# Order of ScalarE's copies, the second maximum and VectorE's normalisation in a five-stage attention kernel

## The reference

```python
def attn(xq, xc, Wq, Wk, Wv, Wo, bo):            # 16 heads of 64
    q, k, v = xq @ Wq, xc @ Wk, xc @ Wv          # by heads
    return softmax(q k^T * 64 ** -0.5) v @ Wo + bo

x = attn(ln(x, g1, b1), ln(x, g1, b1), ...) + x   # SELF
x = attn(ln(x, g2, b2), ctx, ...) + x             # CROSS
x = (a * gelu(gate)) @ Wf + bf + x                # GEGLU; a, gate = split(ln(x, g3, b3) @ Wp + bp)

q, k, v = x @ Wq + bq, ctx @ Wk + bk, ctx @ Wv + bv   # CROSS2, 16 heads of 8
out = softmax(q k^T * 8 ** -0.5) v @ Wo + bo
h = gelu((ln(out) * g + b) @ W1 + b1)              # FFN
return x + out + h @ W2 + b2
```

## Time and profile before

| | |
|---|---|
| median of the runs | 475.29 us |
| the profiled execution | 476.33 us, its span 474.6 us |
| TensorE matmuls busy | 457.4 us, 96% |
| VectorE busy | 361.2 us, 76% |
| ScalarE busy | 281.6 us, 59% |
| GpSimd busy | 193.2 us, 41% |
| mean granted TensorE clock | 0.993 |

### The profile page before, as it was taken

How to read it: one execution, slowest core, us unless ns; L and a number is a source line. 1 busy time by engine, 2 the same in 40 slices (tenths; PEclk the granted TensorE clock), 3 DMA queues, 4 the chain that set the end, 5 groups by cost and what they waited for, 6 DMA issues and landing times.

```text
span 474.6 us, 17652 instructions
## 1 busy us (share of the span) xinstructions
PE 457.4 (96%) x7650; PEld 416.3 (88%) x7650; DVE 361.2 (76%) x654; ACT 281.6 (59%) x505; POOL 193.2 (41%) x216
## 2 busy tenths in 40 slices
PE   7779999999999999999999999998999999998897
PEld 7779898998998989989899898998999787777797
DVE  4868788787877887878878788796885678688562
ACT  4455654766546666566565654754554567676773
POOL 3642433445523535435442443334351323132483
PEclk9979999999999999999999999999999999999999
DMA  7101120310200000000000000000000000000011
GB/s 225 44 5 49 35 80 4 74 47 3 59 5 1 11 12 1 12 7 5 12 3 11 11 1 11 3 3 2 2 0 8 19 10 18 2 2 1 1 44 45
DMA packets 17300, 10.57 MB, mean 22 GB/s; under 512 B 7888, under 2 KB 16272, under 8 KB 17232
## 3 DMA queue, kind: packets, MB, share of 16 engines
q1 hardware_dynamic: 16800, 9.48, 7.3%
q10 hardware_dynamic: 432, 0.07, 0.1%
HBM read 8.50 MB, written 1.05 MB: 20 GB/s over the span
## 4 chain that ended last, share of the span: by engine, by line
PE 84%; DVE 10%; ACT 2%; issue 2%; POOL 1%; DMA 1%; DVEq 0%; ACTq 0%; POOLq 0%
PE out0p L774 13%; PE stage L593 12%; PE stage L594 11%; PE stage L595 11%; PE stage L755 7%; PE scp L680 7%; PE scp L725 6%; PE scp L895 6%; DVE mx L1182 3%; PE out0p L790 2%; PE scp L696 2%; DVE vb L1159 1%; PE stage L608 1%; PE stage L808 1%; DVE pr L1177 1%
## 5 line engine op out<-in xcount | busy, mean ns | idle before, releaser
L1439 POOL TENSOR_TENSOR pr<-pr,rc 128x1024 f32<-128x1024 f32 x32 | 60.9, 1904 | 91.5 <-DVE rc L1207 91.4
L774 PE MATMUL out0p<-wo_of,ot 128*128 128x128 f32 x512 | 68.1, 281 | 0.0
L774 PEld LDWEIGHTS out0p<-wo_of,ot 128*128 128x128 f32 x512 | 60.8, 191 | 2.1
L972 ACT ACTIVATE pr<-pr 128x1024 f32<-128x1024 f32 x48 | 50.7, 1056 | 14.8 <-DVE pr L1177 12.2
L916 ACT ACTIVATE q_of_heads<-stage 128x512 f32<-128x512 f32 x48 | 28.4, 595 | 50.7 <-PE stage L595 49.0
L916 ACT ACTIVATE vt<-stage 64x512 f32<-64x512 f32 x64 | 37.9, 592 | 28.1 <-PE stage L595 26.5
L1212 DVE COPY vt<-stage 64x512 f32<-64x512 f32 x64 | 44.4, 694 | 4.5 <-PE stage L595 1.9
L1205 DVE TENSOR_REDUCE sm<-pr 128x16 f32<-128x1024 f32 x32 | 38.9, 1217 | 7.9 <-ACT pr L972 7.9
L1172 DVE TENSOR_REDUCE mx<-scp 128x16 f32<-128x1024 f32 x32 | 38.2, 1195 | 6.7 <-PE scp L680 6.7
L680 PEld LDWEIGHTS scp<-k_of_heads,q_of_heads 64*64 64x64 f32 x2048 | 33.1, 134 | 8.5 <-ACT ot L916 5.5
L1177 DVE TENSOR_TENSOR pr<-scp,mx 128x1024 f32<-128x1024 f32 x32 | 39.2, 1224 | 1.1
(11 more groups left out here) (237 smaller groups left out, 1284.3 us busy)
## 6 DMA issues: line engine op xcount, KB each, us to landing
ctx_in<-in_ctx_dram SPq DMA_DIRECT2D x16, 96.0 KB, 2.0
wo_of<-in_L_xattn_Wo_dram SPq DMA_DIRECT2D x2, 512.0 KB, 4.1
out_dram<-rows SPq DMA_DIRECT2D x8, 128.0 KB, 1.8
rows<-in_x_dram SPq DMA_DIRECT2D x1, 768.0 KB, 9.5
pr<-in_L_xattn_Wq_dram SPq DMA_DIRECT2D x1, 512.0 KB, 4.7
pr<-in_L_xattn_Wk_dram SPq DMA_DIRECT2D x1, 512.0 KB, 6.3
pt<-in_L_xattn_Wv_dram SPq DMA_DIRECT2D x1, 512.0 KB, 7.7
rows<-in_L_xattn_Wq_dram SPq DMA_DIRECT2D x1, 512.0 KB, 3.5
```

The costliest lines, as they stand in the source:

```text
L774: last = nc.tensor.matmul(out0p[:, t * D:(t + 1) * D], ot[:, a // 2, a % 2, t, :], wo_w[s.phase][:, a, :], start=(a == 0), stop=(a == PAIR ...
L972: nc.scalar.activation(pr[t][:, :], pr[t][:, :], ACT.Exp, scale=scale[s.phase]).then_inc(exped, 1)
L1439: nc.gpsimd.tensor_tensor(halves(pr[t][:, :]), halves(pr[t][:, :]), rc[:, t, :, None].to_broadcast([ROWS, H, N]), ALU.mult).then_inc(probs, 1)
```

## The change

Three orders change; no instruction is added or taken away.

- ScalarE, SELF group 0: the copies of projections 2 to 6 of the next group go ahead of the second exp, not behind it.
- VectorE, SELF group 0: the second maximum goes ahead of the first sum; the second sum goes behind the copy of projection 7.
- VectorE, CROSS2, all groups: the normalisation of the group before and the v bias of the next group go ahead of the second maximum, in this order; before, the order was second maximum, v bias, normalisation.

```diff
--- before.py
+++ after.py
@@ -1027,10 +1027,10 @@
                         pt_step(s, 0)
                         p_step(one, (1,))
                     else:
+                        p_step(one, (0,) if before else range(1, 7))
+                        exp_step(s, 1)
                         if before:
-                            p_step(one, (0,))
-                        exp_step(s, 1)
-                        p_step(one, range(1, 8))
+                            p_step(one, range(1, 8))
                         val_step(s, (0, 1))
                         pt_step(s, 0)
                         val_step(s, (2,))
@@ -1246,10 +1246,12 @@
                     shift_step(s, 0)
                     if before:
                         av_step(before, 1)
+                        sum_step(s, 0)
+                        max_step(s, 1)
                     else:
                         p_step(one, range(4))
-                    sum_step(s, 0)
-                    max_step(s, 1)
+                        max_step(s, 1)
+                        sum_step(s, 0)
                     shift_step(s, 1)
                     if last:
                         val_step(s, (0, 1))
@@ -1263,7 +1265,7 @@
                     stats_step(two)
                     if last:
                         p_step(one, (0,))
-                    else:
+                    elif before:
                         sum_step(s, 1)
                     if last:
                         val_step(s, (2,))
@@ -1271,6 +1273,8 @@
                         p_step(one, (1,))
                     else:
                         p_step(one, range(4, 8))
+                        if not before:
+                            sum_step(s, 1)
                         val_step(s, (0, 1))
                         pt_step(s, 0)
                         val_step(s, (2,))
@@ -1289,11 +1293,11 @@
                         stats_step(two)
                     cross2_max_step(s, 0)
                     cross2_shift_step(s, 0, before)
-                    cross2_max_step(s, 1)
+                    if before:
+                        cross2_norm_step(before)
                     if not last:
                         p_step(one)
-                    if before:
-                        cross2_norm_step(before)
+                    cross2_max_step(s, 1)
                     cross2_shift_step(s, 1, before)
                     if two.phase == FFN:
                         norm_step(two, one)
```

## The result

The changed kernel takes 471.02 us (median of 4 runs, 470.87 to 471.22), the kernel before 475.22 (median of 4). The ratio is 0.9911, with a 95% interval of 0.9894 to 0.9929: faster by 4.2 us, where 7.2 were forecast, and 0.2 us above the upper end of the range. The profiled execution took 471.22 us, its span is 469.5.

What follows compares the result with a forecast made beforehand. TensorE, busy 96% of the span, was taken as the bound. From the 475.29 us median, 4.7 in the first group and 2.5 in CROSS2, together 7.2, gave 468.1 us, range 466.9 to 470.8.

Steps and rivals of the forecast that it cites:

- Copies, second maximum, second exp: SELF group 0: copies from 20.6 on, second maximum at 20.19, second exp at 24.0; TensorE not stopping at 21.90.
- what is late next: SELF group 0: TensorE would wait up to 2 us for GpSimd's second probabilities and start their transposes at 29.0.
- Behind it the order is the old one: After the first group's second transposes: old order, needed copies older than 29.5, so the 4.7 us gain is kept.
- The 4.7: First group's gain in us: second transposes at 29.0 in place of 33.72, bounds 4.3 and 4.9.
- The rival: First group: the clock falls in TensorE's new wait, costing up to 2.5 us, time 470.6; chance 0.10.
- VectorE's share of the first group: SELF group 0: second shift 0.5 earlier, second sum at 25.5 behind projection 7's copy, against 25.61 before.
- 0.3, 0.3, 1.4, 0.7 and -0.2: CROSS2 gains in us: group 0, group 1, four loop groups at 0.35 each, group 6, and a loss in group 7.
- 0.37: CROSS2 loop group: transposes of `att` at 393.42 in place of 393.79, 0.37 us earlier.
- shift 1 takes the place of `att`: CROSS2: second shift 0.4 later than reckoned, groups 0 to 5 give nothing, CROSS2 gains 0.5, time 470.1; chance 0.13.
- The weighed rule: CROSS2, second maximum to second shift: the skill implies no adjacency delay; the sum kept the trace's 0.1 later start.
- the low end of CROSS2: CROSS2 gaining only 0.5 us of the forecast 2.5.
- the sum's own range: Whole kernel: time by the bounds of both parts, 467.3 to 470.5 us.

Runs made afterwards that it cites:

- the first-group run: The changed kernel with CROSS2 put back in its old order, leaving the first group's orders changed, against the kernel before: 472.51 us, ratio 0.9938.
- the run with the late v bias: The changed kernel with CROSS2's v bias behind the second maximum again and the normalisation left ahead: 480.5 us, one run.

## Why the prediction was wrong

Direction, bound and places were right. The size was not: 4.2 where 7.2 stood, and outside the range.

- **Copies, second maximum, second exp: right.** Each start lies within 0.1 of the working, and so does "what is late next": GpSimd's probabilities at 28.9, TensorE waiting 2.13.
- **"Behind it the order is the old one": the step that failed first.** The 4.7 was taken at the start of the transposes and carried to the end. Behind a 2.1 us wait it shrinks by 1.5 when the clock falls, in 10 of 14 executions, and in all four of the changed kernel. The rival stood in the text with 0.10, because the new wait was shorter than the time from the beginning of the old one to its fall. That was no reason: in the new kernel the fall came at 30.5, 3.7 us from the wait's beginning, when TensorE had been busy for 1.5. The Trainium skill (TensorE: Matmul & The Clock Gate, section "HAM oscillation — how this bites in real kernels"), cited beside the rival, says that a wait of TensorE can throttle its clock so that the next burst starts cold. The trace agrees that a wait, here of 2.13 us, can lower the clock, and differs in the rest: the burst behind it started at 1.00 and fell 1.5 us later. The rival's price was 2.5 in the text and is 1.5 in the traces, where only 3.4 us are at the low clock.
- **VectorE's share of the first group: its sign was missed.** The working found the second sum 0.1 earlier and never asked what the third value product then does. It fills the wait if the sum goes first, and leaves it in one piece if the copy does. ScalarE's hunk alone gives 4.2, close to the forecast of 4.7; the orders of VectorE added to it take 1.4 away. The second sum behind the copy is the order that does it: with that sum ahead again, the whole change gives 6.3.
- **CROSS2: mechanism right, terms mis-sized.** The sum said 0.3, 0.3, 1.4, 0.7 and -0.2, 2.5 in all. The scores of groups 0, 1, 6 and 7 start at 366.37, 373.69, 416.58 and 424.93, and at 370.06, 377.63, 421.55 and 430.43 before. From one group's scores to the next the traces show gains of 0.25, 0.16, 4 x 0.21, 0.53 and -0.32, together 1.5. In the loop group 0.37 was worked out from the transposes of `att`. The reciprocal started 4.14 behind the scores and not 4.08; of this 0.04 is that the out product stands later behind the scores, and the profile puts that down to the second exp, which holds the transposes behind the scores (the 0.42 of idle weight loads at 384.26, released by ScalarE). The half set of transposes behind a wait took 0.49 and not 0.43, and the scores came 0.67 behind L808 and not 0.64: 0.16 less. So the rival "shift 1 takes the place of `att`" was true to at most that small part, through the exp. That the end of shift 1 and the scores would come within 0.1 of each other was nearly right: 391.42 and 391.55.
- **The weighed rule.** The second shift starts 0.04 behind the end of the maximum that it waits for (388.93 + 1.22, then 390.19), while the second sum, which waits for nothing by then, starts 0.08 before the end of the copy in front of it (24.81 + 0.68, then 25.41). The trace has the 0.1 that the sum had. The section that was weighed against it (the Trainium skill, VectorE: DVE Perf Modes, "The DRAIN you can't avoid") goes on to say that an instruction that isn't held starts earlier, which the prediction left out and which agrees with these rows.
- **The difference of the two profiles is 5.1 us, and the medians differ by 4.2.** The profiled execution of before lies 1.1 above its median, the one of after 0.2. In the former 0.45 sits in the CROSS phase, where the programs are the same: from the closing products at 157.75 to those at 177.59 it is 19.84 us, and 19.38 in the changed kernel. A sum made against one execution carries that. Its mean clock is 0.993, with 6.8 us at the low clock. The 16 of 37 executions with 0.996 are about 1 us shorter; no trace of one was kept, so how much less such an execution has to gain stays open.
- **The range.** Its upper end took in the rival of the clock or the low end of CROSS2, each alone. The clock fell and CROSS2 gave 1.0 less at the same time. With the traces' terms, 4.8 less 1.5 in the first group and 1.5 in CROSS2, the sum is 470.5; the other 0.5 lies within the interval of the measurement. A slip of rounding beside it: the low end of the sum's own range is 475.29 - 4.9 - 3.0 = 467.4, not 467.3.

## What to carry to other kernels

When a stall of TensorE is shortened but not removed, price the work behind it at the half clock too, and look for an order that breaks the rest of the stall with work that is due anyway: here one wait of 2.13 us cost, in most executions, 1.5 us more than 0.99 and 0.41 with a product in between. Try each hunk alone: one of the three here carried the first group's whole gain, another turned part of it back. An engine's step that sets a PSUM bank free (the v bias here) is on the path of whoever writes that bank next, so it has to move with what is moved past it.

## What the runs showed of the hardware

- The granted clock can fall after the wait is over. In the changed kernel TensorE had been busy for 1.5 us when it went to 0.50, in the first-group run, behind a wait of 1.85 us, for 0.3 us; the program was the same up to there. It stayed low for 3.4 us in both, and for 6.8 us in the kernel before.
- A wait of 2.13 us was followed by the fall in the changed kernel's trace and not in that of the run with the old order in the last group, whose first group is the same. By the mean clock, executions of that one program are of both kinds: 469.17 and 469.83 us with 1.000, 470.68 and 470.69 with 0.996.
- In the run with the late v bias the clock fell in CROSS2, where TensorE's waits for the v bias are 1.3 us long and come some 10 us apart: 0.50 between 404 and 405.
- One float32 product of 128 x 128 by the identity stands as two instructions in the trace and took 0.23 us at the full clock (32 in 3.73 us).
